# The band mask of the windowed attention as a GpSimd product between two exponentials, instead of a matmul with the identity

## The reference

```
scores = einsum('bhqd,bhkd->bhqk', q, k) / sqrt(dh)          # 16 heads, dh = 16
scores = exp(scores - max(scores, axis=-1))                  # maximum over all 1024 keys
mask   = (j - i <= 31) & (j - i >= -32)
scores = where(mask, scores, 0.0)
weights = softmax(scores, axis=-1)                           # a second exponential: outside the band exp(0) = 1
out = einsum('bhqk,bhkd->bhqd', weights, v) @ Wo
x = layernorm(x + out)
x = layernorm(x + leaf_layer(x))                             # per-row choice of one of 16 leaves, for q, k and v, then attention
```

## Time and profile before

| | us |
|---|---|
| median of 3 runs | 2041.89 (2038.99 to 2049.73) |
| the profiled execution | 2045.43 |
| its span (first to last instruction) | 2043.6 |
| PE busy | 1794.1 (88%) |
| PEld busy | 1334.9 (65%) |
| DVE busy | 1602.4 (78%) |
| ACT busy | 1342.1 (66%) |
| POOL busy | 898.5 (44%) |

### The profile page before, as it was taken

How to read it: one execution, slowest core, us unless ns; L and a number is a source line. 1 busy time by engine, 2 the same in 40 slices (tenths; PEclk the granted TensorE clock), 3 DMA queues, 4 the chain that set the end, 5 groups by cost and what they waited for, 6 DMA issues and landing times. The chain is left out here.

```text
span 2043.6 us, 49487 instructions
## 1 busy us (share of the span) xinstructions
PE 1794.1 (88%) x16304; PEld 1334.9 (65%) x16304; DVE 1602.4 (78%) x4371; ACT 1342.1 (66%) x2643; POOL 898.5 (44%) x1338
## 2 busy tenths in 40 slices
PE   3989999999999999999999636878888699999997
PEld 2546556565565565565655526777787589999997
DVE  2788998988979979989889536978886477777775
ACT  2798898888888878888888315757664244344342
POOL 4323433566555645655565552000303755555411
PEclk8999999999999999999999658999998899999999
DMA  6443536446455464465354629888874333333211
GB/s 215 125 121 97 159 110 176 132 125 178 150 135 158 128 192 123 145 188 159 108 151 121 166 95 299 260 251 307 273 229 151 107 89 96 91 96 96 83 39 39
DMA packets 207317, 304.84 MB, mean 149 GB/s; under 512 B 48429, under 2 KB 108890, under 8 KB 207066
## 3 DMA queue, kind: packets, MB, share of 16 engines
q1 hardware_dynamic: 157322, 195.73, 32.7%
q0 software_dynamic: 29440, 68.98, 11.9%
q10 hardware_dynamic: 20304, 36.97, 4.9%
HBM read 104.16 MB, written 115.87 MB: 108 GB/s over the span
## 5 line engine op out<-in xcount | busy, mean ns | idle before, releaser
L1487 DVE CUSTOM_DVE_ANT_0 above<-p_half,above 128x512 f32<-128x512 f32 x1024 | 680.3, 684 | 102.0 <-ACT above L1171 79.7
L1171 ACT ACTIVATE above<-p_diff 128x512 f32<-128x512 f32 x1024 | 593.7, 600 | 88.8 <-PE p_diff L1047 85.7
L1047 PE MATMUL p_diff<-d_stack,q_stack 96*128 96x512 bf16 x1024 | 392.8, 386 | 30.2 <-ACT above L1171 15.7
L1051 PE MATMUL p_half<-k_stack,q_stack 96*128 96x512 bf16 x1024 | 388.7, 382 | 22.0 <-DVE row_max L1487 20.9
L1809 POOL DMA_INDIRECT raw<-sorted_y,slot x192 | 202.8, 1056 | 348.7 <-DMA sorted_y<-y_tile 293.6
L222 POOL DMA_INDIRECT sorted_x<-y,slot x192 | 198.6, 1035 | 95.9 <-issue 48.9
L2056 ACT ACTIVATE pt_hi<-p_one 128x512 fp32r<-128x512 f32 x128 | 69.5, 595 | 246.2 <-PE p_one L1932 246.2
L1192 ACT ACTIVATE w_win<-p_win 128x512 f32<-128x512 f32 x256 | 153.9, 601 | 50.1 <-PE p_win L1072 45.2
L1047 PEld LDWEIGHTS p_diff<-d_stack,q_stack 96*128 96x128 bf16 x1024 | 98.6, 98 | 110.9 <-ACT above L1171 49.3
L1051 PEld LDWEIGHTS p_half<-k_stack,q_stack 96*128 96x128 bf16 x1024 | 100.5, 99 | 96.6 <-DVE row_max L1487 78.3
L1200 ACT ACTIVATE w_win<-w_win 128x512 f32<-128x512 f32 x256 | 163.3, 638 | 0.2
(11 more groups left out here) (277 smaller groups left out, 4824.6 us busy)
## 6 DMA issues: line engine op xcount, KB each, us to landing
sorted_x<-zeros SPq DMA_DIRECT2D x141, 256.0 KB, 3.0
x_tile<-sorted_x SPq DMA_DIRECT2D x141, 256.0 KB, 4.1
sorted_y<-y_tile ACTq DMA_DIRECT2D x141, 256.0 KB, 3.6
q_stack<-q_parts SPq DMA_DIRECT2D x256, 96.0 KB, 2.4
k_stack<-k_parts SPq DMA_DIRECT2D x256, 96.0 KB, 2.4
d_stack<-d_parts SPq DMA_DIRECT2D x256, 48.0 KB, 2.0
v_win<-v_tiles POOLq DMA_DIRECT2D x16, 544.0 KB, 6.0
v_win<-v_tiles POOLq DMA_DIRECT2D x32, 272.0 KB, 6.8
```

The lines of the kernel that those rows point to most:

```text
L1047: nc.tensor.matmul(p_diff[s % 2][:], qs, d_stack[0:SPLIT_ROWS, h, :], start=True, stop=True).then_inc(s_diff, 1)
L1051: nc.tensor.matmul(p_half[s % 3][:], qs, k_stack[0:SPLIT_ROWS, h, HALO + S // 2:HALO + S], start=True, stop=True).then_inc(s_half, 1)
L1171: nc.scalar.activation(above[:, s % 4], p_diff[s % 2][:], ACT.Relu).then_inc(s_above, 1)
L1487: nc.vector.tensor_tensor_reduce(out=above[:, s % 4], in0=p_half[s % 3][:], in1=above[:, s % 4], scale=1.0, scalar=-3.0e38, op0=ALU.add, o ...
```

## The change

The matmul with `outside` goes. In its place there is a tile `inside` of f32, ones in the band and zeros outside it, and GpSimd multiplies `w_win` by it after the first exponential. So the value outside the band becomes 0 there, where it was exp(-30000 ...) = 0 before. The padding stays on PE; its matmul now starts the accumulation in the edge block, and the other blocks start with their own product. The product on GpSimd stands at lags 29 and 32, between the split of k, d or q and the scatter of that step. The second exponential moves from lags 29 and 32 to 31 and 35 and waits for the product.

```
-EXP_LAGS, EXP2_LAGS = (28, 31), (29, 32)
+EXP_LAGS, MASK_LAGS, EXP2_LAGS = (28, 31), (29, 32), (31, 35)
...
-        outside = sb("outside", [P, WIN], BF16)
+        inside = sb("inside", [P, WIN])
...
-            const(nc.gpsimd.memset(outside[:], 0.0))
+            const(nc.gpsimd.memset(inside[:], 1.0))
...
-            const(nc.gpsimd.affine_select(out=outside[:], in_=outside[:], compare_op=ALU.is_ge, fill=OUTSIDE,
+            const(nc.gpsimd.affine_select(out=inside[:], in_=inside[:], compare_op=ALU.is_ge, fill=0.0,
...
+                    for half in (0, 1):
+                        for w, o, h in late(b, g, s, MASK_LAGS[half]):
+                            keep_inside(GH * w + h, h, half)
                     for r, n, t in scatters(b, g, s):
...
+            def keep_inside(k, h, half):
+
+                pool.wait_ge(s_e1, 2 * k + half + 1)
+                weights = w_win[:, h % 2, NBLK // 2 * half:NBLK // 2 * half + NBLK // 2, 0:WIN]
+                nc.gpsimd.tensor_tensor(weights, weights, inside[:].unsqueeze(1).to_broadcast([P, NBLK // 2, WIN]),
+                                        ALU.mult).then_inc(s_inside, 1)
...
-                nc.tensor.matmul(p_win[:].rearrange("p (i j) -> p i j", j=WIN), ident_b[:],
-                                 outside[:].unsqueeze(1).to_broadcast([P, NBLK // 2, WIN]),
-                                 start=True, stop=False, skip_group_check=True)
                 edge = slice((512 - WIN) * half, (512 - WIN) * half + WIN)
                 nc.tensor.matmul(p_win[:, edge], ident_b[:], pads[:, half:half + 1].to_broadcast([P, WIN]),
-                                 start=False, stop=False, skip_group_check=True)
+                                 start=True, stop=False, skip_group_check=True)
...
                     ins = nc.tensor.matmul(p_win[:, WIN * n:WIN * n + WIN], k_stack[0:ROWS, h, WIN * i:WIN * i + P],
-                                           q_stack[0:ROWS, h, WIN * i:WIN * i + WIN], start=False,
-                                           stop=n == NBLK // 2 - 1, skip_group_check=True)
+                                           q_stack[0:ROWS, h, WIN * i:WIN * i + WIN], start=i not in (0, NBLK - 1),
+                                           stop=True, skip_group_check=True)
...
-                act.wait_ge(s_e1, 2 * k + half + 1)
+                act.wait_ge(s_inside, 2 * k + half + 1)
```

More of the change, by code:

```diff
@@ L80 @@
 TURN_AT = 4
-OUTSIDE = -30000.0
+PADDING = -30000.0
 STATS_LAGS = 3, 4, 5
@@ L366, in window_attention @@
         s_e1 = sem("first_exp")
+        s_inside = sem("first_exp_inside_the_window")
         s_ww = sem("window_weights")
@@ L664, in _ @@
             pool.wait_ge(s_const, 14)
-            const(nc.gpsimd.memset(pads[0:HALO, 0:1], OUTSIDE))
-            const(nc.gpsimd.memset(pads[P - HALO:P, 1:2], OUTSIDE))
+            const(nc.gpsimd.memset(pads[0:HALO, 0:1], PADDING))
+            const(nc.gpsimd.memset(pads[P - HALO:P, 1:2], PADDING))
             pool.wait_ge(s_const, 16)
```

## The result

The change makes the kernel slower by a tenth: 2257.83 us median of 4 runs (2254.42 to 2261.02) against 2040.44 for the kernel before, ratio 1.105 (95% interval 1.102 to 1.107). The forecast was 2089, with a range up to 2145. So the sign was right and the size was not.

What follows compares the result with a forecast made beforehand. It took the hand-on between PE, ScalarE and VectorE as the bound, no engine being full. Stops of 62 us less 15 of credit gave +47 on the median 2041.9, so 2089 us; range 2030 to 2145.

Steps and rivals of the forecast that it cites:

- 62 us of stops: Attention stage: late GpSimd products stop ScalarE, 93 us over odd, even and light units, less a third: 62 us.
- credit: PE loses 256 mask matmuls of 0.22 us; only where ScalarE waited for PE does it count: 15 us gained.
- the recovery: A third of the 93 us comes back, through ScalarE being often a slot ahead and VectorE's idle time.
- The product's duration: GpSimd's 128x512 f32 product: 1.16 us, taken from L720, the nearest row with two inputs.
- The linear scaling to 3.04: The small f32 product's 0.285 us scaled by 512/48; GpSimd full, kernel near 2450 us; chance 2 in 100.
- the walk: GpSimd's order followed through the second half of the odd unit at 652.9: products 4.2, 2.9 and 8.0 us late.
- The size of the stops: Largest lateness is about a unit's loss: 8 us in odd, 5.5 in even, 3.5 in light units; sum 93.
- The port rival: VectorE instructions with two SBUF inputs locked out by GpSimd's products: 12 us more, 2101, or 88, 2177; chance 0.05.
- rival 4: GpSimd becomes the bound in loaded units, its splits and maxima late as well: 2143 us; chance 0.17.

Runs made afterwards that it cites:

- experiment "short": The changed kernel with GpSimd's product over one block of eight (64 of 512 columns), the rest not masked: 2194.88 us, ratio 1.027.
- the late variant: The changed kernel with the second exponential at lags 35 and 38 instead of 31 and 35: 2176.82 us, ratio 1.018.
- the unread variant: The kernel before, plus a GpSimd product (384 columns) into a spare tile that nobody reads: 2138.52 us, ratio 1.001.
- the control: The kernel before, unedited, run again with a trace of its own on the chip of the later runs: 2145.19 us, ratio 1.000.

## Why the prediction was wrong, step by step

- **The sum, term by term.** Forecast were 62 us of stops (93 less a third) and 15 of credit. The idle time of ScalarE has +155 for the stops, +62 ahead of the rectifier where -31 had been taken for the recovery, and -30 for the credit. Of the 140 us between +47 and +187, the stops are 62, the recovery is 93, and the credit takes 15 off. So two steps failed: the size of the stops and, the larger, the recovery.
- **The credit** was forecast at 15 us; without any mask it is 8. Right in kind: ScalarE's wait ahead of the first exponential fell from 50 to 21 us in the changed kernel, though there the stops hide it.
- **The product's duration** was taken as 1.16 us from L720; it is 1.189. Right. The linear scaling to 3.04 was far off, and the small product of experiment "short" (64 columns, 0.319) shows the fixed part.
- **The place of the stops** was right for the walk: the products behind a set of maxima and a split. The walk began in the middle of the unit, and so it missed that heads 5 and 7 stand two steps behind a set as well. There are four such places in a unit, and the largest stops are those of heads 1, 3 and 7.
- **The size of the stops: the first step that failed.** The prediction had "the largest lateness is about what a unit loses, not the sum of them", and in the odd unit a lateness that grows to 8.0 us. The sum was 93 us; the trace has 155. There is no such growing lateness. The odd unit shown above has three large stops, of 3.9, 3.4 and 3.9 us, and between them GpSimd is in time again: its products wait for the first exponential, 197.5 us in all. The next set of maxima makes it late anew. So a unit loses several stops of 1 to 4 us, 6 to 10 us together in each of the first fourteen, with scatters or without: the windows of the first five units, which have none, wait 38 us for the product where I gave them 17. The run with the maxima moved behind the product took three quarters of these stops away and so shows that the maxima make them.
- **"I take a third back": the second step that failed, and the larger one.** Nothing came back. The rectifier's waits for PE went up by 62 us, where the recovery would have needed them to go down. VectorE's idle time did not take the stops in: it stood 258 us for ScalarE, where it had stood 79.7.
- **The term that was missing** is TensorE's clock. In the rows the prediction used it stood at 1.00 in all three units, and I did not ask what keeps it there. During a stop of PE of 2.9 us it fell, and it stood at 0.51 for 7 us. Its share of the loss is not shown. The rule is in the Trainium skill (TensorE: Matmul & The Clock Gate, "Part 1: The HAM clock gate"): the engine is throttled by default, and only recent activity of its own lifts that. The trace agrees, by the 0.51 from that stop on.
- **The port rival** (0.05) has some support, as an addition to the forecast. A normalisation on VectorE took 1.33 us beside a product, where it takes 0.40; in the late variant the longest took 2.78. (The difference of `d_parts`, with two inputs in SBUF, had a median of 1.28 us there, where it has 0.68 in both kernels.)

```profile
789.02 1.33 DVE L1476 TENSOR_SCALAR y<-y,mean_var,rstd 128x256 f32<-128x256 f32 x1
```

  VectorE's busy time was 42 us higher in the unread variant than in the control (1645.2 against 1603.6), and this may be what its first five units lost; no run takes the two apart. In the changed kernel it was 26 us above the kernel before (1628.4 against 1602.4). I had named only instructions with two inputs in SBUF; the normalisation has one.
- **GpSimd as the bound** (rival 4, 0.17) came nearest in its number, 2143, but not as the main mechanism: GpSimd is busy 58 of 86 us, and nearly the same use of it, unread, cost 10 of the 52 to 57 us in the first five units.
- **Not foreseen at all** was that the order of ScalarE's list costs 0.9% by itself.
- **What stays open:** why the same change is 1.105 at first and 1.062 later. The kernel before has stops of all three engines in its later trace that its first trace does not have, and kernels with the product have hardly any.

## What to carry to other kernels

When work moves to an engine with free time, its free time is not the question: ask what stands ahead of the work in that engine's list, and how many steps its reader leaves it. A stop in a tightly coupled loop was not averaged out here, and it recurred at each place where the list has the same order. Add to the stop what it does to TensorE's clock: read that column in the kernel before, and treat "1.00" as a thing that a stop can take away.

When the kernel to compare with has disturbances of its own, compare a stretch that is free of them too. Here it changed the reading of two experiments: two ratios of 1.00 hid 10 and 13 us in the first five units.

## What the runs showed of the hardware

- TensorE's granted clock fell to its lower level during a stop of 2.9 us of PE and came back 7 us later (790.2 to 797 us above); this also happened in the later trace of the kernel before, after a stop with another cause. It fell with shorter stops too: 8 of the 43 falls in the changed kernel have no long wait for the product near them, and the longest stop of PE around these is 1.0 to 2.2 us.
- GpSimd's product of two f32 inputs takes 1.189 us for 512 columns and 0.319 for 64, so, by an estimate from these two, 1.94 ns a column and 0.195 us fixed.
- VectorE's `tensor_scalar` with one f32 input in SBUF, 128x256, took 1.33 us instead of 0.40 where it started 0.03 us behind a GpSimd product, while L1487 with one of its inputs in PSUM kept a mean of 684 ns in both kernels.
- The kernel before took 2040 us in the first measurement and 2134 to 2146 on four chips later, the changed kernel 2258 and 2281. The first five units took 325.5 and 326.7 us in the two traces of the kernel before.
